# Two depooling stages written out in groups of four tiles

## The chip, the cores and the metric

The kernel runs on one core of one Trainium2 chip. The metric is the device time of one execution in microseconds. Engine names: PE (TensorE), DVE (VectorE), ACT (ScalarE), POOL (GpSimd), SP (SyncE, which issues the DMAs here).

## What is computed

The network has twelve blocks, in four layers of three, on an `x` of 128 sequences x 32 positions x 128 features; each block adds its result to `x`. Blocks `L0_xattn` (the first) and `L3_xattn` (the tenth) are the "depooling" blocks:

```python
def _hnet_depool(h, h_patch_full, patch_lens):
    ...
    _, s = jax.lax.associative_scan(comb, (a_b, u), axis=1)   # decaying sum over the patches
    depool = s.reshape(bsz, plen, D_MODEL)
    plug = jnp.clip(jnp.cumsum(boundary_mask, axis=1) - 1, 0, plen - 1)
    depool_out = depool[jnp.arange(bsz)[:, None], plug]       # one row per position
    return depool_out + h
h = rmsnorm(embeds, g_res)
h = jnp.einsum('bld,ed->ble', h, W_in) + b_in
h_patch = rmsnorm(patch_embeds, g_init)
return _hnet_depool(h, h_patch, patch_lens)
...
x = x + _L0_xattn_ref(_layernorm(x, axis=-1), ctx_2048, mask_BxS2_if0, L0_xattn_W_in, ...)
```

`embeds` is the layer-normalised `x`; `patch_embeds` comes from `ctx_2048` alone.

## The kernel before, in words

`x` stays in SBUF for the whole program as `core.x`, 32 tiles of 128 rows (4 sequences x 32 positions) by 128 features. A first piece of code, `start`, prepares what both depooling stages share: `core.ctx_n`, the normalised context rows, and `core.depool`, for each tile the 128x128 matrix that does scan and gather in one matmul. Then the twelve stages run one after another. Each has its own block of code per engine, and a barrier stands between two stages: no engine works ahead into the next one. Inside a stage the engines run their own queues in written order and meet only at semaphores. The profile cuts the leading `L0` or `L3` of a tile's name to `L`, so `L_xattn_patch` is that of either depooling stage, by its time.

A depooling stage, `depool_cross`, does for each tile: mean and variance (`dve_moments`, DVE lines L119 and L122); the inverse root, which is both normalisations in one, as four small operations on POOL (`pool_rstd`, L135, L138, L140, L142); `(x - mean) * rstd` on DVE (`dve_normalise`, L147), a 128x128 operation per tile; a transpose on PE (L153), copied by ACT out of PSUM four tiles at a time (L160); two matmuls per tile into the same PSUM region, `depool` matrix times `patch` (L417) and transposed tile times `w` (L418); and `x_b` plus that sum into `x` on DVE, four tiles at a time (L398). `patch` is `ctx_n * g_init`, on POOL (L365), and `x_b` is `x + b_in`, on POOL (L369); both treat four tiles (128x512) per instruction. ACT copies the matrices of four tiles into `mat` (L382) ahead of the matmuls.

The tiles go in four rounds of eight (`S = 8`), three in a hardware loop (`over_steps`) and the last written out. DVE and POOL wait at the start for all four loads (`w_in`, 64), and DVE first scales `w` by `g_res` (L388). Within a round POOL does `patch` twice, `x_b` twice and then the roots of the next round; DVE does the moments and the normalising of the next round and then this round's two additions.

A later stage, `lora_experts` (`L3_ffn`, called the expert stage below), is untouched by the change. It is written out in groups of four tiles and adds a bias in place on POOL (L2882).

Of the kernel before, what the change touches and what calls it, by code (L numbers as in the profile page):

```python
# [328 lines left out]
def depool_cross(core, name):  # L329

    nc, dram = core.nc, core.dram
    S, PACK = 8, 4
    with ExitStack() as st:
# [4 lines left out]
        x_b = sb("x_b", [P, S, D])  # L338
        g_init = sb("g_init", [P, D])
        mat = sb("mat", [P, S, P])  # L340
        patch = sb("patch", [P, S, D])
        front = Front(core, st, name, S, lambda s: core.psum[:, s // PACK, s % PACK * P:s % PACK * P + P], rms=True,
                      pack=PACK)
        out = lambda u: core.psum[:, 2 + u, :].rearrange("p (s d) -> p s d", d=D)
        w_in, w_done, copied, patch_done, x_b_done, out_done, added = (core.sem(f"{name}_{n}") for n in (
            "w_in", "w_done", "copied", "patch_done", "x_b_done", "out_done", "added"))
        block = st.enter_context(nc.Block())
        U = S // PACK

        @block.sync  # L350
        def _(sp):
            load(sp, [(w[:, :], dram[f"{name}_W_in_T"]), (g_res[:, :], dram[f"{name}_g_res"]),
                      (b_in[:, :], dram[f"{name}_b_in"].to_broadcast([P, D])),
                      (g_init[:, :], dram[f"{name}_g_init"][:, 0:D].to_broadcast([P, D]))], w_in)

        @block.gpsimd
        def _(pool):
            pool.wait_ge(w_in, 64)
            b4 = b_in[:, :].rearrange("p (s d) -> p s d", s=1).to_broadcast([P, PACK, D])
            g4 = g_init[:, :].rearrange("p (s d) -> p s d", s=1).to_broadcast([P, PACK, D])  # L360
            def step(it, more):
                for u in range(U):

                    pool.wait_ge(out_done, it * U + u + 1)
                    nc.gpsimd.tensor_tensor(patch[:, 4 * u:4 * u + 4, :], core.ctx_n[:, ds(it * S + 4 * u, PACK), :], g4,  # L365
                                            ALU.mult).then_inc(patch_done, 1)
                for u in range(U):
                    pool.wait_ge(added, it * U + u + 1)
                    nc.gpsimd.tensor_tensor(x_b[:, 4 * u:4 * u + 4, :], core.x[:, ds(it * S + 4 * u, PACK), :], b4,  # L369
                                            ALU.add).then_inc(x_b_done, 1)  # L370
                if more:
                    front.pool_rstd(pool, (it + 1) * S)
# [2761 lines left out]
```

## Time and profile before

| | us |
|---|---|
| median of 3 runs | 4280.81 (4277.31 to 4282.16) |
| the profiled execution | 4273.29 |
| its span, first to last instruction | 4271.1 |
| first depooling stage, first load to end of last addition | 63.15 to 116.20 |
| second depooling stage | 4044.84 to 4098.95 |

In the profile a time is counted from the span's start. Busy time of an engine leaves out waits; "idle before" an instruction, in brackets, names what ended the wait. The two depooling stages are 107 of 4271 us; PE is busy 81% of the whole span, DVE 63%, POOL 28%.

### The profile page before, as it was taken

Reading aid. Unit: us, or ns where it says so; the run is one execution under the profiler, and the core shown is the slowest. Engines: PE = TensorE matmul, PEld = TensorE weight load, DVE = VectorE, ACT = ScalarE, POOL = GpSimd, SP = SyncE. Lnnn points to the kernel's source line nnn. Section 1 sums busy time; section 2 is a strip of 40 time slices with the busy share of each in tenths; the row PEclk is TensorE's granted clock in tenths of the full one; section 3 lists DMA queues with packets and bytes.
Section 4 is the critical chain, followed back from the end, with each engine's and each line's share of the span. In section 5 each row is a group of like instructions: output and inputs, shape, how many; then the busy total and the mean of one; then the engine's idle time right before and its main releaser. Section 6 shows DMA issues by size and latency. Waiting matters only on the chain. (4 is left out here: it accounts for less than half of the span.)

```text
span 4271.1 us, 82785 instructions
## 1 busy us (share of the span) xinstructions
PE 3473.3 (81%) x26877; PEld 2960.9 (69%) x26885; DVE 2688.3 (63%) x7468; ACT 1765.1 (41%) x4503; POOL 1202.9 (28%) x1644
## 2 busy tenths in 40 slices
PE   3787788888868888777769999999999999872634
PEld 2676777777756666445559999999999999642334
DVE  6773888888857888564235545555555554477667
ACT  1230666666637777554113323333332332222542
POOL 2551766676623333202000000000000000153021
PEclk8995999999989999988669999999999999876666
DMA  3000000000012222100111111111111111162000
GB/s 84 4 0 32 1 0 0 0 0 0 0 32 71 77 75 75 41 5 0 31 39 46 51 40 50 46 45 45 45 51 40 50 46 46 32 108 47 2 0 22
DMA packets 262344, 147.46 MB, mean 35 GB/s; under 512 B 110327, under 2 KB 258763, under 8 KB 261614
## 3 DMA queue, kind: packets, MB, share of 16 engines
q1 hardware_dynamic: 257742, 140.55, 12.4%
q10 hardware_dynamic: 4512, 5.77, 0.6%
q8 instruction: 49, 0.80, 0.1%
q14 instruction: 41, 0.34, 0.0%
HBM read 131.82 MB, written 13.65 MB: 34 GB/s over the span
## 5 line engine op out<-in xcount | busy, mean ns | idle before, releaser
L901 PE MATMUL psum<-L_ffn_share,L_ffn_prob 128*128 128x128 f32 x4096 | 511.2, 284 | 141.5 <-DVE L_ffn_prob L830 141.5
L901 PEld LDWEIGHTS psum<-L_ffn_share,L_ffn_prob 128*128 128x128 f32 x4096 | 491.3, 198 | 173.5 <-DVE L_ffn_prob L830 141.9
L2074 ACT ACTIVATE L_xattn_prob<-psum,L_xattn_nmax 128x258 f32<-128x258 f32 x512 | 238.6, 471 | 677.3 <-DVE L_xattn_nmax L2109 677.3
L725 POOL TENSOR_TENSOR L_ffn_sums<-L_ffn_sims 128x1024 f32<-128x1024 f32 x256 | 485.5, 1911 | 107.6 <-DVE L_ffn_prob L830 107.3
L2186 PE MATMUL psum<-L_xattn_ctxT,L_xattn_q_ctx 128*128 128x257 f32 x2048 | 488.8, 381 | 0.0
L2224 PE MATMUL psum<-L_xattn_probT,L_xattn_ctx 128*128 128x256 f32 x2048 | 484.6, 380 | 1.7 <-DVE L_xattn_probT L2127 1.7
L830 DVE SCALAR_TENSOR_TENSOR L_ffn_prob<-L_ffn_sums,L_ffn_best,psum 128x512 f32<-128x512 f32 x512 | 358.2, 740 | 105.2 <-ACT psum L758 101.2
L2127 DVE COPY L_xattn_probT<-psum 128x512 f32<-128x512 f32 x256 | 176.9, 691 | 392.0 <-PE psum L2210 392.0
L2186 PEld LDWEIGHTS psum<-L_xattn_ctxT,L_xattn_q_ctx 128*128 128x128 f32 x2048 | 370.9, 191 | 48.2
L2049 POOL TENSOR_TENSOR L_xattn_z_var<-L_xattn_z_mv,L_xattn_z_eps 128x1 f32<-128x1 f32 x32 | 6.1, 190 | 1398.0 <-DVE L_xattn_z_mv L2141 1365.3
L2224 PEld LDWEIGHTS psum<-L_xattn_probT,L_xattn_ctx 128*128 128x128 f32 x2048 | 370.2, 191 | 42.0 <-ACT L_xattn_lastT L2085 2.2
L758 ACT ACTIVATE psum<-L_ffn_sums,L_ffn_bias 128x512 f32<-128x512 f32 x512 | 337.1, 683 | 136.2 <-DVE L_ffn_prob L830 136.1
L1189 ACT ACTIVATE L_xattn_prob<-psum,L_xattn_nmax 128x289 f32<-128x289 f32 x512 | 249.5, 500 | 125.5 <-DVE L_xattn_nmax L1216 125.5
L2090 ACT COPY L_xattn_mixed_ctx<-psum 128x512 f32<-128x512 f32 x256 | 149.7, 585 | 362.1 <-PE psum L2224 362.1
L2171 PEld LDWEIGHTS psum<-L_xattn_xnT,L_xattn_m_h 128*128 128x128 f32 x2048 | 273.3, 197 | 23.4 <-DVE L_xattn_q_ctx L2101 9.7
L2171 PE MATMUL psum<-L_xattn_xnT,L_xattn_m_h 128*128 (+1 forms) x2048 | 279.9, 281 | 8.6 <-DVE L_xattn_q_ctx L2101 7.0
L2195 PEld LDWEIGHTS psum<-L_xattn_u_h,L_xattn_mixed_ctx 128*128 128x128 f32 x2048 | 233.5, 192 | 2.9 <-ACT L_xattn_mixed_ctx L2090 1.1
L2195 PE MATMUL psum<-L_xattn_u_h,L_xattn_mixed_ctx 128*128 128x128 f32 x2048 | 233.9, 275 | 0.7 <-ACT L_xattn_mixed_ctx L2090 0.7
L1216 DVE TENSOR_REDUCE L_xattn_nmax<-psum 128x1 f32<-128x289 f32 x512 | 198.9, 450 | 45.9 <-PE psum L1256 45.8
L2101 DVE COPY L_xattn_q_ctx<-psum 128x512 f32<-128x512 f32 x256 | 174.7, 682 | 38.3 <-PE psum L2171 38.3
L2109 DVE TENSOR_REDUCE L_xattn_nmax<-psum 128x2 f32<-128x516 f32 x256 | 177.9, 695 | 20.5 <-issue 2.9
L2117 DVE TENSOR_SCALAR L_xattn_prob<-L_xattn_prob,L_xattn_total 128x256 f32<-128x256 f32 x512 | 158.5, 351 | 20.0
(426 smaller groups left out, 6629.0 us busy)
## 6 DMA issues: line engine op xcount, KB each, us to landing
L_xattn_ctxT<-ctx_T_dram SPq DMA_DIRECT2D x128, 257.0 KB, 2.8
L_xattn_ctx<-ctx_dram SPq DMA_DIRECT2D x128, 256.0 KB, 3.0
L_xattn_k_all<-ctx_T_dram SPq DMA_DIRECT2D x128, 128.5 KB, 2.1
L_xattn_v_all<-ctx_dram SPq DMA_DIRECT2D x128, 128.0 KB, 2.2
L_attn_qkv_scratch<-L_attn_qkv SPq DMA_DIRECT2D x24, 256.0 KB, 2.9
L_attn_rows<-L_attn_qkv_scratch SPq DMA_DIRECT2D x24, 256.0 KB, 5.3
start_raw<-ctx_dram ACTq DMA_DIRECT2D x16, 256.0 KB, 12.2
start_plug_all<-plug_scratch SPq DMA_DIRECT2D x1, 2048.0 KB, 6.7
```

What stands on the lines that cost most here:

```text
L725: nc.gpsimd.tensor_tensor(sums[:, h % RING, :, :], sx, sy, ALU.add).then_inc(summed, 1)
L758: nc.scalar.activation(raw_prob(k), half(sums[:, h % RING, :, :].rearrange("p i j -> p (i j)"), k), ACT.Exp, bias=bias[:, s, h:h + 1]).the ...
L830: nc.vector.scalar_tensor_tensor(half(prob[:, h % RING, :], k), half(sums[:, h % RING, :, :].rearrange("p i j -> p (i j)"), k), best[:, s, ...
L901: last = nc.tensor.matmul(pair(2 * s)[:, c * P:(c + 1) * P], prob[:, h % RING, c * P:(c + 1) * P], share[:, h % RING, :], start=(h == 0 an ...
L1189: ins = nc.scalar.activation(prob[:, b % 2, g, :], scores(g), ACT.Exp, bias=nmax[:, b % 2, g:g + 1], accum_out=total[:, b % 2, g:g + 1])
L1216: nc.vector.tensor_reduce(nmax[:, b % 2, g:g + 1], scores(g), X, ALU.max, negate=True).then_inc(maxed, 1)
L2074: ins = nc.scalar.activation(prob[:, s, g, :], scores(s)[:, g, :], ACT.Exp, bias=nmax[:, s, g:g + 1], accum_out=total[:, s, g:g + 1])
L2109: nc.vector.tensor_reduce(nmax[:, u % 2, :], scores(u % 2), X, ALU.max, negate=True).then_inc(maxed, 1)
L2171: last = nc.tensor.matmul(Q[:, i * P:(i + 1) * P], m_h[:, 4 * j + i, c * P:(c + 1) * P], tokens(t), start=True, stop=True)
L2186: last = nc.tensor.matmul(scores(s)[:, g, 0:CTX], q_ctx[:, p, c, b, h:h + 4, :].rearrange("p h n -> p (h n)"), ctxT[:, b, c, :], start=(c ...
L2195: nc.tensor.matmul(OUT, mixed_ctx[:, c, h, :], u_h[:, c, h, :], start=(c + h == 0), stop=False)
L2224: last = nc.tensor.matmul(dst, ctx[:, b, k, c * P:(c + 1) * P], probT[:, s, k, :], start=(k == 0), stop=(k == 1))
```

## The change

Only `depool_cross` is edited; both depooling stages use it. Eight groups of four tiles are written out without a loop. `front` has slots for all 32 tiles, so no buffer of the normalised tiles is used twice. The loads come in another order on two semaphores: `g_init` and `b_in` (`rows_in`, for POOL), then `w` and `g_res` (`w_in`, for DVE). DVE takes moments at once and scales `w` behind the normalising of group 0. POOL takes the roots of groups 0 and 1 by themselves and later ones over pairs of groups; it adds the bias to `x` in place once the group is normalised, and `x_b` is gone. PE reads `core.depool` in place, so `mat` and ACT's copies are gone. PE transposes group g+1 ahead of the product of group g, and group g's addition stands on DVE behind the normalising of group g+2.

```diff
-    S, PACK = 8, 4
+    S = 4
+    GROUPS = TILES // S
...
+        patch = sb("patch", [P, TILES, D])
+        xnT = sb("xnT", [D, 3, S, P])
+        front = Front(core, st, name, TILES, None, transposed=False, rms=True)
+        turn_bank = lambda g: core.psum[:, g % 2, :].rearrange("p (s w) -> p s w", s=S)
+        out_bank = lambda g: core.psum[:, 2 + g % 2, :].rearrange("p (s d) -> p s d", d=D)
...
+            load(sp, [(g_init[:, :], dram[f"{name}_g_init"][:, 0:D].to_broadcast([P, D])),
+                      (b_in[:, :], dram[f"{name}_b_in"].to_broadcast([P, D]))], rows_in)
+            load(sp, [(w[:, :], dram[f"{name}_W_in_T"]), (g_res[:, :], dram[f"{name}_g_res"])], w_in)
...
+            def patches(g):
+                nc.gpsimd.tensor_tensor(patch[:, g * S:(g + 1) * S, :], core.ctx_n[:, g * S:(g + 1) * S, :], over(g_init),
+                                        ALU.mult).then_inc(patch_done, 1)
+
+            def add_bias(g):
+                pool.wait_ge(front.normed, (g + 1) * S)
+                nc.gpsimd.tensor_tensor(x_of(g), x_of(g), over(b_in), ALU.add).then_inc(biased, 1)
+
+            front.pool_rstd(pool, 0, only=tiles(0))
+            front.pool_rstd(pool, 0, only=tiles(1))
+            pool.wait_ge(rows_in, 32)
+            patches(0)
+            patches(1)
+            for g in range(2, GROUPS, 2):
+                front.pool_rstd(pool, 0, only=pair(g))
+                add_bias(g - 2)
+                patches(g)
+                add_bias(g - 1)
+                patches(g + 1)
+            add_bias(GROUPS - 2)
+            add_bias(GROUPS - 1)
...
+            for g in range(GROUPS):
+                act.wait_ge(front.turned, (g + 1) * S)
+                if g >= 3:
+                    act.wait_ge(out_done, g - 2)
+                nc.scalar.copy(xnT[:, g % 3, :, :], turn_bank(g)).then_inc(xnT_done, 1)
...
-            dve.wait_ge(w_in, 64)
...
+            def add(g):
+                dve.wait_ge(out_done, g + 1)
+                dve.wait_ge(biased, g + 1)
+                nc.vector.tensor_tensor(x_of(g), x_of(g), out_bank(g), ALU.add).then_inc(added, 1)
+
+            front.dve_moments(dve, 0, only=tiles(0))
+            front.dve_moments(dve, 0, only=tiles(1))
+            front.dve_normalise(dve, 0, only=tiles(0))
+            dve.wait_ge(w_in, 32)
             nc.vector.tensor_scalar(w[:, :], w[:, :], g_res[:, :], None, ALU.mult).then_inc(w_done, 1)
...
+            for g in range(1, GROUPS + 2):
+                if g % 2 and g + 2 < GROUPS:
+                    front.dve_moments(dve, 0, only=pair(g + 1))
+                if g < GROUPS:
+                    front.dve_normalise(dve, 0, only=tiles(g))
+                if g >= 2:
+                    add(g - 2)
...
+            def turn(g):
+                if g >= 2:
+                    pe.wait_ge(xnT_done, g - 1)
+                for s in range(S):
+                    pe.wait_ge(front.normed, g * S + s + 1)
+                    nc.tensor.transpose(turn_bank(g)[:, s, :], front.xn[:, g * S + s, :],
+                                        core.c("ident")).then_inc(front.turned, 1)
+
+            def out(g):
+                pe.wait_ge(patch_done, g + 1)
+                if g >= 2:
+                    pe.wait_ge(added, g - 1)
+                pe.wait_ge(xnT_done, g + 1)
+                for s in range(S):
+                    nc.tensor.matmul(out_bank(g)[:, s, :], core.depool[:, g * S + s, :], patch[:, g * S + s, :], start=True,
+                                     stop=False)
+                    last = nc.tensor.matmul(out_bank(g)[:, s, :], xnT[:, g % 3, s, :], w[:, :], start=False, stop=True)
+                last.then_inc(out_done, 1)
+
+            turn(0)
             pe.wait_ge(w_done, 1)
+            for g in range(GROUPS):
+                if g + 1 < GROUPS:
+                    turn(g + 1)
+                out(g)
```

How the rows move. On DVE at the head of the stage, before: scaling of `w` (L388), moments and normalising of eight tiles, then the loop.

```order
L388 TENSOR_SCALAR L_xattn_w<-L_xattn_w,L_xattn_g_res 128x128
L119 BN_STATS L_xattn_front_stats_sb<-x_sb 128x6 x8
L122 BN_AGGR L_xattn_front_mv_sb<-L_xattn_front_stats_sb 128x2 x8
L147 TENSOR_SCALAR L_xattn_front_xn_sb<-x_sb,L_xattn_front_mv_sb,L_xattn_front_rstd_sb 128x128 x8
L179 UNCONDITIONAL_BRANCH
```

The same place in the changed kernel (L403 scales `w`, L397 is the addition into `x`):

```order
L119 BN_STATS L_xattn_front_stats_sb<-x_sb 128x6 x4
L122 BN_AGGR L_xattn_front_mv_sb<-L_xattn_front_stats_sb 128x2 x4
L119 BN_STATS L_xattn_front_stats_sb<-x_sb 128x6 x4
L122 BN_AGGR L_xattn_front_mv_sb<-L_xattn_front_stats_sb 128x2 x4
L147 TENSOR_SCALAR L_xattn_front_xn_sb<-x_sb,L_xattn_front_mv_sb,L_xattn_front_rstd_sb 128x128 x4
L403 TENSOR_SCALAR L_xattn_w<-L_xattn_w,L_xattn_g_res 128x128
L119 BN_STATS L_xattn_front_stats_sb<-x_sb 128x6 x8
L122 BN_AGGR L_xattn_front_mv_sb<-L_xattn_front_stats_sb 128x2 x8
L147 TENSOR_SCALAR L_xattn_front_xn_sb<-x_sb,L_xattn_front_mv_sb,L_xattn_front_rstd_sb 128x128 x8
L397 TENSOR_TENSOR x_sb<-x_sb,psum 128x512
```

Moments of two groups now stand ahead of everything, and `w` behind group 0; the eight L147 in a row are groups 1 and 2, with no addition between them.

On POOL, one pass of the loop before: `patch` (L365) and `x_b` (L369) of a round, then the roots of the next.

```order
L365 TENSOR_TENSOR L_xattn_patch<-ctx_n,L_xattn_g_init 128x512
L364 REGISTER_ALU
L365 ISA
L365 TENSOR_TENSOR L_xattn_patch<-ctx_n,L_xattn_g_init 128x512
L369 REGISTER_ALU
L369 TENSOR_TENSOR L_xattn_x_b<-x_sb,L_xattn_b_in 128x512
L369 REGISTER_ALU
L369 TENSOR_TENSOR L_xattn_x_b<-x_sb,L_xattn_b_in 128x512
L134 ISA
L135 TENSOR_TENSOR L_xattn_front_var_sb<-L_xattn_front_mv_sb,eps 128x8
```

In the changed kernel, from the root over groups 2 and 3 to the next root (L363 is `patches`, L368 `add_bias`):

```order
L142 TENSOR_TENSOR L_xattn_front_rstd_sb<-L_xattn_front_var_sb,minus_half 128x8
L368 TENSOR_TENSOR x_sb<-x_sb,L_xattn_b_in 128x512
L363 TENSOR_TENSOR L_xattn_patch<-ctx_n,L_xattn_g_init 128x512
L368 TENSOR_TENSOR x_sb<-x_sb,L_xattn_b_in 128x512
L363 TENSOR_TENSOR L_xattn_patch<-ctx_n,L_xattn_g_init 128x512
L135 TENSOR_TENSOR L_xattn_front_var_sb<-L_xattn_front_mv_sb,eps 128x8
```

The four operations of 128x512 are still between two roots, but the two on `x` now concern the groups before this pair, in place.

## Rows read from the trace of the kernel before

**Rows 1.** Windows by round, first stage: us, busy us of each engine (instructions), TensorE clock.
```profile
63.15:73.00 9.85, 0.00 (x0) 0.00 (x0) 2.57 (x17) 1.14 (x2) 2.21 (x4) 0.50 0.08 20
73.00:84.35 11.35, 7.71 (x39) 6.42 (x40) 8.26 (x24) 1.79 (x3) 7.15 (x9) 0.59 0.00 0
...
105.57:116.20 10.63, 7.49 (x40) 6.11 (x40) 6.53 (x12) 1.39 (x3) 4.97 (x5) 0.84 0.00 0
```

**Rows 2.** Timeline of DVE and POOL, first stage: start us, us, engine, line, operation.
```profile
67.46 0.29 DVE L388 TENSOR_SCALAR L_xattn_w<-L_xattn_w,L_xattn_g_res 128x128 f32<-128x128 f32 x1 [4.57 <-DMA L_xattn_g_init<-L_xattn_g_init_dram]
...
70.36 0.20 POOL L135 TENSOR_TENSOR L_xattn_front_var_sb<-L_xattn_front_mv_sb,eps 128x8 f32<-128x8 f32 x1 [11.92 <-DVE L_xattn_front_mv_sb L122]
...
73.00 2.48 POOL L365 TENSOR_TENSOR L_xattn_patch<-ctx_n,L_xattn_g_init 128x512 f32<-128x512 f32 x2
73.07 5.97 DVE L147 TENSOR_SCALAR L_xattn_front_xn_sb<-x_sb,L_xattn_front_mv_sb,L_xattn_front_rstd_sb 128x128 f32<-128x128 f32 x8 [2.87 <-POOL L_xattn_front_rstd_sb L142]
...
75.44 2.49 POOL L369 TENSOR_TENSOR L_xattn_x_b<-x_sb,L_xattn_b_in 128x512 f32<-128x512 f32 x2
...
84.50 3.96 DVE L147 TENSOR_SCALAR L_xattn_front_xn_sb<-x_sb,L_xattn_front_mv_sb,L_xattn_front_rstd_sb 128x128 f32 x8 [2.88 <-POOL L_xattn_front_rstd_sb L142]
```

**Rows 3.** Normalising instructions (L147), first stage: duration ns min/median/max, first and last start.
```profile
L147 DVE TENSOR_SCALAR L_xattn_front_xn_sb<-x_sb,L_xattn_front_mv_sb,L_xattn_front_rstd_sb x32: 332/335/1303, 73.1 to 109.3; 128x128 f32 x24, 128x128 f32<-128x128 f32 x8
```

**Rows 4.** Timeline, later rounds of the first stage, and the start of the next stage.
```profile
89.22 2.49 POOL L369 TENSOR_TENSOR L_xattn_x_b<-x_sb,L_xattn_b_in 128x512 f32<-128x512 f32 x2 [2.38 <-DVE x_sb L398]
...
89.87 1.64 DVE L119 BATCH_NORM_STATS2 L_xattn_front_stats_sb<-x_sb 128x6 f32 x8 [0.21 <-issue]
...
110.33 0.80 PE L417 MATMUL psum<-L_xattn_patch,L_xattn_mat 128*128 128x128 f32 x2
...
113.72 0.69 DVE L398 TENSOR_TENSOR x_sb<-L_xattn_x_b,psum 128x512 f32<-128x512 f32 x1 [2.85 <-PE psum L418]
...
115.51 0.69 DVE L398 TENSOR_TENSOR x_sb<-L_xattn_x_b,psum 128x512 f32<-128x512 f32 x1 [1.10 <-PE psum L418]
116.47 0.33 SPq L167 DMA_DIRECT2D L_attn_w_qk<-L_attn_Wqk_dram  x1
...
116.57 0.29 DVE L119 BATCH_NORM_STATS2 L_attn_front_stats_sb<-x_sb 128x6 f32<-128x128 f32 x1 [0.38 <-PEq L333]
```

**Rows 5.** Timeline of the expert stage (L3_ffn, last of the program), DVE and POOL.
```profile
4201.42 1.08 DVE L119 BATCH_NORM_STATS2 L_ffn_front_stats_sb<-x_sb 128x6 f32<-128x128 f32 x4 [0.37 <-PEq L2718]
...
4204.43 1.11 DVE L147 TENSOR_SCALAR L_ffn_front_xn_sb<-x_sb,L_ffn_front_mv_sb,L_ffn_front_rstd_sb 128x128 f32<-128x128 f32 x4
...
4215.15 1.46 DVE L147 TENSOR_SCALAR L_ffn_front_xn_sb<-x_sb,L_ffn_front_mv_sb,L_ffn_front_rstd_sb 128x128 f32<-128x128 f32 x2 [0.34 <-POOL L_ffn_front_rstd_sb L142]
...
4203.38 1.01 POOL L142 TENSOR_TENSOR L_ffn_front_rstd_sb<-L_ffn_front_var_sb,minus_half 128x4 f32<-128x4 f32 x1
...
4204.80 1.10 POOL L142 TENSOR_TENSOR L_ffn_front_rstd_sb<-L_ffn_front_var_sb,minus_half 128x4 f32<-128x4 f32 x1
...
4215.01 1.26 POOL L2882 TENSOR_TENSOR x_sb<-x_sb,L_ffn_b_lin 128x512 f32<-128x512 f32 x1
```

**Rows 6.** DMA issues in the first stage's head: line, size, us from issue to landing.
```profile
L_xattn_g_res<-L_xattn_g_res_dram SPq DMA_DIRECT2D x1, 0.5 KB, 2.0
```

**Rows 7.** Windows of PE: us, busy us (instructions), granted clock, DMA share, GB/s.
```profile
99.72:102.60 2.88, 2.88 (x13) 0.50 0.00 0
...
113.10:115.50 2.40, 2.37 (x21) 1.00 0.00 0
```

**Rows 8.** Timeline of the head of the second depooling stage.
```profile
4049.28 0.29 DVE L388 TENSOR_SCALAR L_xattn_w<-L_xattn_w,L_xattn_g_res 128x128 f32<-128x128 f32 x1 [5.71 <-DMA L_xattn_g_init<-L_xattn_g_init_dram]
...
4052.71 0.19 POOL L135 TENSOR_TENSOR L_xattn_front_var_sb<-L_xattn_front_mv_sb,eps 128x8 f32<-128x8 f32 x1 [49.42 <-DVE L_xattn_front_mv_sb L122]
```

**Rows 9.** Windows by round, second stage (columns as in the first group).
```profile
4044.84:4055.41 10.57, 0.00 (x0) 0.00 (x0) 2.57 (x17) 1.14 (x2) 2.27 (x4) 0.52 0.08 19
...
4088.00:4098.95 10.95, 7.67 (x40) 6.38 (x40) 6.54 (x12) 1.79 (x3) 4.98 (x5) 0.84 0.00 1
```

More of the change, by code:

```diff
@@ L347, in depool_cross @@
         block = st.enter_context(nc.Block())
-        U = S // PACK
+        tiles = lambda g: range(g * S, (g + 1) * S)
+        pair = lambda g: range(g * S, (g + 2) * S)
+        x_of = lambda g: core.x[:, g * S:(g + 1) * S, :]
         @block.sync
         def _(sp):
-            load(sp, [(w[:, :], dram[f"{name}_W_in_T"]), (g_res[:, :], dram[f"{name}_g_res"]),
-                      (b_in[:, :], dram[f"{name}_b_in"].to_broadcast([P, D])),
-                      (g_init[:, :], dram[f"{name}_g_init"][:, 0:D].to_broadcast([P, D]))], w_in)
+            load(sp, [(g_init[:, :], dram[f"{name}_g_init"][:, 0:D].to_broadcast([P, D])),
+                      (b_in[:, :], dram[f"{name}_b_in"].to_broadcast([P, D]))], rows_in)
+            load(sp, [(w[:, :], dram[f"{name}_W_in_T"]), (g_res[:, :], dram[f"{name}_g_res"])], w_in)
@@ L356, in _ @@
         @block.gpsimd
         def _(pool):
[L358 to L372, printed above, removed]
@@ L374, in _ @@
-            front.pool_rstd(pool, 0)
-            over_steps(pool, TILES // S, step)
+            over = lambda t: t[:, :].rearrange("p (s d) -> p s d", s=1).to_broadcast([P, S, D])
+            def patches(g):
[4 more added lines that the diff above has]
+                nc.gpsimd.tensor_tensor(x_of(g), x_of(g), over(b_in), ALU.add).then_inc(biased, 1)
@@ L385, in _ @@
         @block.vector
         def _(dve):
-            dve.wait_ge(w_in, 64)
-            nc.vector.tensor_scalar(w[:, :], w[:, :], g_res[:, :], None, ALU.mult).then_inc(w_done, 1)
-            def step(it, more):
-                if more:
-                    front.dve_moments(dve, (it + 1) * S)
-                    dve.wait_ge(front.turned, (it + 1) * S)
-                    front.dve_normalise(dve, (it + 1) * S)
-                for u in range(U):
-                    dve.wait_ge(out_done, (it + 1) * U + u + 1)
-                    x = core.x[:, ds(it * S + 4 * u, PACK), :]
-                    dve.wait_ge(x_b_done, it * U + u + 1)
-                    nc.vector.tensor_tensor(x, x_b[:, 4 * u:4 * u + 4, :], out(u), ALU.add).then_inc(added, 1)
@@ L407, in _ @@
-            pe.sem_inc(added, U)
-            pe.wait_ge(w_done, 1)
-            with pe.Fori(0, TILES // S) as it:
-                front.pe_transpose(pe, it * S)
-                for u in range(U):
-                    pe.wait_ge(added, it * U + u + 1)
-                    pe.wait_ge(copied, it * U + u + 1)
-                    pe.wait_ge(patch_done, it * U + u + 1)
-                    pe.wait_ge(front.xnT_done, it * S + 4 * u + 4)
-                    for s in range(4 * u, 4 * u + 4):
-                        nc.tensor.matmul(out(u)[:, s % 4, :], mat[:, s, :], patch[:, s, :], start=True, stop=False)
-                        last = nc.tensor.matmul(out(u)[:, s % 4, :], front.xnT[:, s, :], w[:, :], start=False, stop=True)
-                    last.then_inc(out_done, 1)
+            def turn(g):
[5 more added lines that the diff above has]
+                                        core.c("ident")).then_inc(front.turned, 1)
```

19 lines of the change are left out of this document (2 added, 17 removed).

## The prediction

> **What bounds the kernel now.** Every stage starts behind a barrier, so only time inside the two depooling stages can move. I read the windows by round first [rows 1]. The first stage lasts from 63.15 to 116.20: 53.05 us, of which 9.85 are a head, 11.35 the first round (from one start of `patch` on POOL to the next), 10.63 the last, which leaves 10.61 for each of the two between. In no round is an engine near full (DVE 8.26 of 11.35), so this is a chain of waits. The head [rows 2] shows DVE doing nothing until 67.46, when the last of four loads has landed; then come moments, the four steps of the inverse root on POOL (from 70.36), and at 73.00 `patch`.
>
> The round is a loop of two engines: the root waits for the moments, the normalising (DVE L147) waits for the root, and the next moments stand behind it on DVE. See L147 in the first round: eight tiles take 5.97 us, beside four POOL operations of 128x512 that run without a gap from 73.00 to 77.93. In the second round, beside two such operations, they take 3.96. The shortest is 0.332 us, the longest 1.303, a POOL operation's length [rows 3], and four tiles beside small POOL operations take 1.11 (4204.43), which is 0.27 from start to start. So while POOL works through 128x512 operands one tile gets through per operation, and the rest follow at 0.27. The count fits twice: 4 x 1.24 + 4 x 0.27 = 6.0, and 2 x 1.24 + 6 x 0.27 = 4.1. Moments are not held: beside the two `x_b` operations of 89.22, eight tiles take 1.64 us in all [rows 4], little more than one of them.
>
> **The change, from POOL's queue.** I write t for the first moment at which DVE can work in a stage, 0.10 us behind the first load, as in the stage that follows (116.57 against 116.47 [rows 4]): 63.25 and 4044.94. P is the start of the 128x512 operations on POOL behind a root over a pair of groups.
>
> *Head.* In the expert stage the first moments of four start at 4201.42 and the root's last step at 4203.38, 0.35 behind its first [rows 5]. So the first root starts at t+1.6; it costs 3 x 0.35 + 1.01 = 2.06, the second as much: they end at t+3.7 and t+5.75. `patches` 0 and 1 add 2.48: t+8.2. Their rows are issued 0.9 us earlier or more than the load that had landed by 67.46, so they are there by t+4. DVE normalises group 0 until t+4.85 and then wants `w` and `g_res`; the latter, issued at about t+1.2, needs 2.0 us [rows 6] and is covered by 1.6. Scaling and the moments of groups 2 and 3 end at t+7.5, under `patches`. The root over this pair takes 2.64 (70.36 to 73.00): P2 = t+10.8, that is 74.05, against 73.00 for the first P of before.
>
> *Rounds.* Behind each pair's root POOL has bias, patch, bias, patch, with nothing to wait for: the biases need tiles normalised a round earlier. That is 4.97 us without a gap, and in it DVE wants the four tiles of the even group. Before, round one alone met four operations, later ones two. By the count above all four tiles are held, to P+5.03. In the expert stage this very operation, `x` plus bias in place behind the same wait, starts at 4215.01, ahead of L147 at 4215.15, whose first two tiles take 1.46 us [rows 5]. So POOL gets in first. Then come the addition (0.67), the moments of the next pair (0.08 + 1.64 + 0.08 + 0.64), 0.09 to POOL and 2.64 for its root: 5.03 + 0.67 + 2.44 + 0.09 + 2.64 = 10.87, and 10.84 since an operation starts 0.03 before its predecessor's recorded end. Before: 10.61. Both handle eight tiles, so writing the pipeline out gains nothing in a round. The odd group's tiles (1.11) and its addition run beside the next root.
>
> *Tail.* From P6: tiles of group 6 done at 5.03; their transposes 0.35; PE has held back group 5's product behind them: 3.35 us at granted clock 0.50, that is 1.2 GHz, as from 110.33 to the addition at 113.72 [rows 4, 7]; transposes of group 7, 0.9; products of 6 and 7 at 1.79 each at clock 1.00, 2.4 GHz, as between the additions of 113.72 and 115.51; last addition 0.73: 13.96 us. Before it was 10.63 from the last P, with eight tiles to normalise but two groups, not three, left for PE.
>
> *Off the path.* ACT's copies of the matrices go; ACT is busy 1.79 of 11.35 us [rows 1], so this is 0, and would stay 0 unless PE had its tiles first. PE gets one new order: group g's product stands behind the transposes of g+1. Group 1's, at the slow clock, ends at P+8.7 and its addition is wanted at P+9.2; were this cover of 0.5 us gone, group 4's tiles still have 1.0 us until the next P. Bias in place costs what `x_b` did (1.26 against 2.49 for two).
>
> *Sum.* First stage: head +1.05, one round less -11.35 (three roots over pairs where there were four), two rounds +0.46, tail +3.33: -6.5 us. Second stage: from `w` at 4049.28 to POOL's first operation at 4052.71 it took 3.43 us [rows 8], against 2.90 in the first; I keep those 0.5. Head (10.57 before [rows 9]) +0.83, round -11.35, rounds +0.46, tail 13.96 against 10.95, +3.01: -7.1. Together -13.6. The profiled execution took 4273.29 us, of which 2.2 lie outside its span of 4271.1; it would become 4259.7. The median stood 7.5 above it, so I forecast 4280.8 - 13.6 = 4267.2 us, -0.32%.
>
> **Bounds of what before does not show.** PE's clock when group 5's product starts: before, a round's first product ran at 0.50 although transposes had just gone ahead [rows 7], and I take the same. High here, the tail is 1.6 us shorter per stage: 4264. Low for group 6 too: 4270. The head may lose 1 us per stage to a late `g_res`, or gain 0.5 once if POOL is on time. The runs of before spread over 4.8 us.
>
> **Rivals.**
> *DVE slips ahead of POOL (9%).* If the tiles were not held, a round would be POOL's 2.64 + 4.97 = 7.6, so -6.5 in two rounds, and the tail 3.8 shorter: another -10.3 per stage, 4247. For it: the order of two ready engines is a matter of 0.1 us. Against it: in both places where both stand ready, 73.00 and 4215.01, POOL has won.
>
> *The root holds the tiles too (9%).* I let tiles run freely beside the root; the four of 4204.43 do, while the root's last step beside them took 1.10 instead of 1.01 [rows 5]. If instead each of POOL's four steps let one tile through and was held by one, the root would cost 1.1 us more in the head and in two rounds, and group 0 would delay the moments by some tenths: 3.5 us a stage, 4274, within 0.2%. The Trainium skill, SBUF — State Buffer, section "Who interferes with whom", has this rule: whoever issues first, GpSimd or a VectorE instruction in a 2-port mode, keeps the shared pair "for the whole instruction". By that rule the 3.5 us would come; the trace agrees with it for 128x512 operations (1.303 us) and not for a root over four columns (1.11 for four tiles).
>
> *Straight code must be fetched (4%), the slower side.* Loops repeat their code; now every group's code is new on DVE, POOL and PE. POOL's 0.5 us at 4052.71, with no releaser but moments long done, may be such a fetch. Were it 0.52 us for each of three engines and 16 groups, 48 stalls on the path would cost 25 us: 4292. From 27 stalls the gain is gone, from 43 the kernel is slower by 0.2%. Against it: the expert stage is written out too, and the chain of its rows from 4201.42 to 4204.80 has no such hole. The Trainium skill, Runtime: NRT & Kernel Launch, section "Instruction fetch mechanics", calls the cost of crossing into the next block of straight code mostly hidden; no run here shows that cost.
>
> *The change doesn't do what it says (4%).* DVE's early start is worth nothing if the head stays bound elsewhere, and the tail could grow by another slow product with its transposes: 4 us per stage given back, 4275, no measurable change.
>
> **How the numbers follow.** The forecast case has 74%. What a measurement of this kernel can tell from no change is about 0.2%, 8.6 us. Range 4256 to 4276: below it lies the first rival, above it the fetch stalls and a little of the last; the middle holds PE's clock, `g_res` and the spread of medians. Faster: most of the 74, the 9 of the first rival: 0.81. Same: 0.15. Slower: 0.04.
>
> **What would show it.** DVE's first moments within 0.2 us of the first load, and `w` scaled without a wait. Four POOL operations without a gap behind each pair's root, beside them L147 at about 4.9 us for four tiles, and 1.1 for odd groups. P to P 10.8 us. Behind the last P three groups' products on PE, the first at clock 0.50. Stage lengths 46.5 and 47. The forecast is wrong if P to P is near 7.6, if odd groups' tiles are long, or if idle time with no releaser appears on DVE, POOL or PE.

## The result, and the profile after

The changed kernel took 4270.03 us (median of 16 runs, 4265.83 to 4276.65), the kernel before 4278.46 us in as many runs beside it (4271.87 to 4282.16). The ratio is 0.9983, with a 95% interval of 0.9975 to 0.999: faster by 0.17%, just short of the 0.2% that I had taken for the least that can be told from no change, and inside the predicted range. The gain is 8.4 us where 13.6 were forecast. The two stages show where it fell short. Windows by round of the first depooling stage of the changed kernel, with columns as in [rows 1], cut at the starts of the 128x512 operations behind each pair's root:

```profile
62.56:73.45 10.89, 3.68 (x15) 3.03 (x16) 7.82 (x41) 1.17 (x2) 8.11 (x14) 0.50 0.07 18
73.45:84.44 10.99, 9.20 (x45) 8.22 (x44) 9.46 (x26) 1.17 (x2) 7.36 (x9) 0.53 0.00 0
84.44:95.43 10.99, 7.37 (x47) 6.21 (x46) 9.44 (x26) 1.17 (x2) 7.36 (x10) 0.84 0.00 1
95.43:108.99 13.56, 9.18 (x61) 8.26 (x59) 9.20 (x12) 1.17 (x2) 7.46 (x7) 0.87 0.01 2
```

The same windows of the second stage, which answer to [rows 9]:

```profile
4047.38:4064.98 17.60, 3.67 (x15) 3.03 (x16) 7.83 (x41) 1.17 (x2) 8.15 (x14) 0.58 0.05 12
4064.98:4075.96 10.98, 8.88 (x51) 7.83 (x49) 9.42 (x26) 1.17 (x2) 7.35 (x9) 0.75 0.01 1
4075.96:4086.94 10.98, 7.13 (x43) 6.11 (x41) 9.43 (x26) 1.17 (x2) 7.34 (x9) 0.84 0.00 1
4086.94:4101.64 14.70, 10.13 (x59) 9.21 (x57) 9.21 (x12) 1.17 (x2) 7.47 (x7) 0.77 0.00 1
```

The first stage went from 53.05 to 46.43 us, as forecast (46.5). The second took 54.26 us, where it had taken 54.11: no gain. Its rounds are those of the first stage, its tail is 1.1 us longer, and its head is 17.60 us long instead of 10.89. The timeline of that head, beside [rows 8] (start us, us, engine, line, operation, and in brackets the idle time ahead and what ended it):

```profile
4047.38 0.35 SPq L167 DMA_DIRECT2D L_xattn_g_init<-L_xattn_g_init_dram  x1
...
4048.43 0.38 DVE L122 BATCH_NORM_AGGREGATE L_xattn_front_mv_sb<-L_xattn_front_stats_sb 128x2 f32<-128x6 f32 x4
...
4049.85 0.38 DVE L122 BATCH_NORM_AGGREGATE L_xattn_front_mv_sb<-L_xattn_front_stats_sb 128x2 f32<-128x6 f32 x4
...
4055.56 0.20 POOL L135 TENSOR_TENSOR L_xattn_front_var_sb<-L_xattn_front_mv_sb,eps 128x4 f32<-128x4 f32 x1 [49.74 <-issue]
...
4057.68 1.12 DVE L147 TENSOR_SCALAR L_xattn_front_xn_sb<-x_sb,L_xattn_front_mv_sb,L_xattn_front_rstd_sb 128x128 f32<-128x128 f32 x4 [7.46 <-POOL L_xattn_front_rstd_sb L142]
```

The moments of both first groups are done at 4050.23, the first group's at 4048.81. Yet POOL starts its root at 4055.56, 8.18 us behind the stage's first load, and the profile names nothing that it waited for ("issue"). In the first stage the same instruction follows its moments at once, 1.51 us behind the first load:

```profile
62.67 0.87 DVE L119 BATCH_NORM_STATS2 L_xattn_front_stats_sb<-x_sb 128x6 f32<-128x128 f32 x4 [0.36 <-PEq L202]
...
64.07 0.20 POOL L135 TENSOR_TENSOR L_xattn_front_var_sb<-L_xattn_front_mv_sb,eps 128x4 f32<-128x4 f32 x1 [6.23 <-DVE L_xattn_front_mv_sb L122]
...
67.19 0.28 DVE L403 TENSOR_SCALAR L_xattn_w<-L_xattn_w,L_xattn_g_res 128x128 f32<-128x128 f32 x1
...
70.75 0.20 POOL L135 TENSOR_TENSOR L_xattn_front_var_sb<-L_xattn_front_mv_sb,eps 128x8 f32<-128x8 f32 x1
```

So 6.67 us of the second stage are a late POOL. Before, the same operation stood 7.87 us behind the first load (4052.71 against 4044.84), but there the moments ended only at 4052.03. In the first stage before, POOL started 0.15 us behind the end of the moments (70.36 against 70.21); here it started 0.68 us behind it. So about 0.5 us of POOL's delay was visible, and the rest lay hidden.

### The profile page after: what moved, and what is told of

The parts are those of the page before. It is cut to its first block and busy times, and to the rows that moved or that the text cites. A ratio compares the mean times of both kernels' runs of the same rounds, so it can differ in the third digit from the quotient of the medians.

```text
span 4274.9 us, 82465 instructions
## 1 busy us (share of the span) xinstructions
PE 3485.5 (82%) x26885; PEld 2971.9 (70%) x26885; DVE 2697.9 (63%) x7468; ACT 1757.4 (41%) x4487; POOL 1209.6 (28%) x1652
```

## The experiments

**Theory S**: behind the quantised stage, whose last POOL work is two all-reduces over the partitions, POOL needs some 7 to 8 us to get ready for ordinary tensor operations. It starts on this when the next such instruction comes up in its queue, behind the barrier. In the list of POOL's instructions two entries `ISA` without operands stand between the two kinds. The one of L91 clears semaphores between stages; the one of L135 stands directly ahead of the root, and the trace has a row for it (below, under "What the delay is"). From the changed kernel (before, the same entries stand at the same places):

```
L2578 ISA L_ffn_most<-L_ffn_peaks 128x1
L2532 UNCONDITIONAL_BRANCH
L91 ISA
L358 UNCONDITIONAL_BRANCH
L135 ISA
L135 TENSOR_TENSOR L_xattn_front_var_sb<-L_xattn_front_mv_sb,eps 128x4
```

The rivals: it is a matter of the moments' timing (theory M), or chance, or POOL must only be woken, or the new code brings it, or something behind the barrier does, such as the clearing of semaphores or a fetch of new code (theory F).

"Stage" below is the time from its first load to the next stage's first load, in the profiled execution; POOL is its first tensor operation behind the second stage's first load. Each group of ratios was measured beside the kernel before, on one chip.

| kernel | first stage | second | POOL | ratio (95%) |
|---|---|---|---|---|
| before | 53.32 | 54.38 | 7.87 | |
| changed | 46.69 | 54.53 | 8.18 | 0.9983 (0.9975 to 0.999) |
| e0, changed again | 46.64 | 54.30 | 8.19 | 0.9989 (0.998 to 0.9998) |
| e1, small op early | 47.69 | 46.41 | 1.52 | 0.9977 (0.9967 to 0.9988) |
| e2, before + small op | 54.36 | 53.34 | 7.17 | 1.0003 (0.9994 to 1.0013) |
| e3, weights first | 50.35 | 54.58 | 8.23 | 0.9993 (0.9984 to 1.0003) |
| e4, tiles ahead of biases | 43.80 | 47.22 | 7.56 | 0.9968 (0.9957 to 0.9979) |
| e5, e1 and e4 | 44.13 | 42.69 | 1.51 | 0.9945 (0.9931 to 0.9959) |
| e6, first stage only | 46.56 | 54.08 | 8.08 | 0.9987 (0.9978 to 0.9996) |
| e7, second stage only | 53.66 | 53.24 | 8.26 | 1.0002 (0.9993 to 1.0011) |
| e8, e5 and the tail's tiles | 39.48 | 39.41 | 1.51 | 0.9936 (0.9923 to 0.995) |
| e9, odd product first | 44.96 | 53.37 | 8.16 | 0.9981 (0.9971 to 0.999) |
| e10, e8 and e9 | 39.45 | 39.36 | 1.51 | 0.9944 (0.9931 to 0.9958) |
| e11, small op late | 46.41 | 53.07 | 7.93 | 0.9983 (0.9973 to 0.9993) |

**e0: the changed kernel once more.**

> The changed kernel once more, to see what repeats. In its first profile the first depooling stage took 46.4 us (53.05 before), the second 54.3 (54.1 before), since POOL's first operation there came 6.7 us behind the moments; the rotary stage between them took 232.0 us against 222.7, with the granted clock of PE lower in several windows. If POOL's lateness is built into the program it repeats within 0.2 us; if it was chance it goes. The rotary stage's 9 us I take for chance: it should come out elsewhere between 222 and 233. The ratio to before should lie near 0.998.

POOL is late by the same amount (8.19), so it is not chance. In e4, whose stage has the same head, it starts after 7.56 us, so the delay is not the same to the tenth in every run.

**e1: a small POOL operation directly behind the all-reduces.**

```diff
+        scrap = sb("scrap", [P, 1])
...
             nc.gpsimd.partition_all_reduce(most[:, 3:4], peaks[:, 3:4], P,
                                            bass.bass_isa.ReduceOp.max).then_inc(most_h, 1)
+            nc.gpsimd.tensor_tensor(scrap[:, :], core.eps[:, :], core.half[:, :], ALU.mult)
```

> A one-column POOL operation is added behind the last all-reduce of the stage ahead of the second depooling stage, where POOL is idle for 40 us. Theory S (switch): an instruction that makes POOL ready for ordinary operations again after an all-reduce stands just ahead of its next ordinary operation, costs 7 to 8 us, and is now on the path; the added operation draws it forward. Then POOL's first root starts within 0.2 us of the moments, the second stage takes 46.5 to 47.2 us, and the kernel is 6.5 to 7.5 us faster than the changed one. Theory F (fetch of new code, or the clearing of semaphores, behind the barrier): nothing moves, second stage 54.3 us.

POOL's timeline, from the last all-reduce into the second depooling stage:

```profile
4002.72 0.37 POOL L2579 PARTITION_ALL_REDUCE L_ffn_most<-L_ffn_peaks  x1 [69.17 <-DVE L_ffn_peaks L2672]
4009.89 0.18 POOL L2581 TENSOR_TENSOR L_ffn_scrap<-eps,minus_half 128x1 f32<-128x1 f32 x1 [6.80 <-issue]
4047.82 0.20 POOL L135 TENSOR_TENSOR L_xattn_front_var_sb<-L_xattn_front_mv_sb,eps 128x4 f32<-128x4 f32 x1 [37.75 <-DVE L_xattn_front_mv_sb L122]
```

The idle time without a releaser has moved to the small operation (6.80 us), where POOL has nothing else to do for 38 us. The root now names its real releaser, the moments, and comes 1.52 us behind the first load. The second stage takes 46.41 us, 8.1 less than in the changed kernel; 6.7 of it are POOL, the rest is the tail (13.55 against 14.97 to the next stage's first load). Since the delay now passes ahead of the barrier and the root behind it is on time, nothing behind the barrier causes it, and theory F falls.

In device time the gain was smaller than the expected 6.5 to 7.5 us: the median is 4264.72 us, against 4267.59 for the changed kernel measured beside it (e0), 2.9 us less, and the intervals of the two ratios overlap. In the profiled execution the first stage's tail was 1.1 us longer than in the changed kernel, at PE's low clock, but the tail of one execution doesn't explain a median of nine. That the 6.7 us are gone is shown by the second stage's own length; that they reach the kernel's time in full is not shown by this run alone.

**e11: the same operation, but behind the barrier.**

```diff
+        scrap = sb("scrap", [P, 1])
...
         def _(pool):
...
+            nc.gpsimd.tensor_tensor(scrap[:, :], core.eps[:, :], core.half[:, :], ALU.mult)
```

> The changed kernel with the same small POOL operation as in e1_small_op_early, but as POOL's first instruction inside each depooling stage, behind the barrier and ahead of the first root, with nothing to wait for. Theory S (POOL starts to get ready for tensor operations when its first instruction of the stage comes up, behind the barrier, and needs until about 8 us behind the stage's first load): the small operation itself ends only 7.6 to 8.3 us behind the first load, the root stands behind it, the second stage stays at 54 to 55 us and the ratio at 0.9985. Rival (POOL must only be woken by any operation that doesn't wait for DVE): the small operation runs within 1 us of the first load, the root at 1.5 us, the second stage is 46.5 us and the ratio 0.9975.

```profile
4043.18 0.35 SPq L167 DMA_DIRECT2D L_xattn_g_init<-L_xattn_g_init_dram  x1
...
4051.11 0.18 POOL L371 TENSOR_TENSOR L_xattn_scrap<-eps,minus_half 128x1 f32<-128x1 f32 x1 [51.09 <-issue]
4051.26 0.19 POOL L135 TENSOR_TENSOR L_xattn_front_var_sb<-L_xattn_front_mv_sb,eps 128x4 f32<-128x4 f32 x1
```

An operation that waits for nothing starts 7.93 us behind the first load. So the delay falls on the first tensor operation behind the all-reduces, also on one that waits for nothing; where it stands decides whether it costs anything. The second stage, 53.07 us, is 0.9 below the 54 to 55 that I expected; its tail was 13.61 us against the changed kernel's 14.97.

**e2: the small operation in the kernel before.** Same edit as e1.

> The kernel before, with the same small POOL operation behind the second all-reduce of the quantised stage as in the run e1_small_op_early. Theory S (POOL needs about 8 us from the barrier until its first tensor operation, and before this lay behind the late load of w and the moments but for half a microsecond): the second stage goes from 54.4 to about 53.9 us, as the first (53.3) has it, and the kernel's time does not change (ratio within 0.9985 to 1.0005). Rival (the small operation saves its 8 us in any kernel, for instance by making the barrier come earlier): the second stage about 46.5 us and the kernel at 0.998.

The second stage is 1.04 us shorter, 0.70 of it in POOL's start, and the kernel's time did not change. (The first stage, which the edit doesn't touch, came out 1.04 us longer, so a difference of this size in one profile means little.) POOL still starts 7.17 us behind the first load, but now it is the moments that it waits for: the cover itself is this long.

**e3: loads first, as before.** DVE waits for `w` and `g_res` ahead of the first moments.

```diff
+            dve.wait_ge(w_in, 32)
             front.dve_moments(dve, 0, only=tiles(0))
             front.dve_moments(dve, 0, only=tiles(1))
             front.dve_normalise(dve, 0, only=tiles(0))
-            dve.wait_ge(w_in, 32)
```

> One part of the change undone: DVE waits for the weights ahead of the first moments, as before. First stage: the fourth load lands 3.5 to 4.0 us behind the start, so the head and the stage grow by about that: 50.0 to 50.6 us. Second stage under theory S: POOL is not ready until 8.2 us behind the stage's first load, and the moments of group 0 end at 5.5, still earlier; no change, 54.3 us. If instead POOL's lateness runs from the moment the moments are done (theory M), the second stage also grows by 4, to 58.

```profile
4048.60 0.35 SPq L167 DMA_DIRECT2D L_xattn_g_init<-L_xattn_g_init_dram  x1
...
4052.56 0.87 DVE L119 BATCH_NORM_STATS2 L_xattn_front_stats_sb<-x_sb 128x6 f32<-128x128 f32 x4 [5.24 <-DMA L_xattn_g_res<-L_xattn_g_res_dram]
...
4056.83 0.19 POOL L135 TENSOR_TENSOR L_xattn_front_var_sb<-L_xattn_front_mv_sb,eps 128x4 f32<-128x4 f32 x1 [49.80 <-issue]
```

In the first stage the early moments are worth 3.7 us (50.35 against 46.69). In the second they are worth nothing: moments 3.9 us later, POOL at 8.23 as ever. Theory M expected 58 us there; it took 54.58.

**e6 and e7: the new code in one stage, the loop in the other.**

> The new code in the first depooling stage, the old loop in the second. Theory S: the whole gain of the change sits in the first stage: 46.6 us there and 54.4 in the second, the kernel as fast as with both changed (ratio to the kernel before 0.9985, -6.7 us). Rival (the second stage's new code does gain, and something else of the program pays it back): about half of the changed kernel's gain, ratio 0.999 to 1.0.

> The old loop in the first depooling stage, the new code in the second. Theory S: first stage 53.3 us, second 54.4 (POOL's first tensor operation 8.2 us behind the stage's first load), ratio to the kernel before 1.000 within 0.0007. Rival (the late POOL of the changed kernel comes from the new code in the first stage, which leaves other things loaded): POOL on time, second stage about 47 us, ratio 0.9985.

The whole gain sits in the first stage (0.9987), and the second alone gives none that can be told (1.0002, 0.9993 to 1.0011). In e6 the root of the second stage, at 8.08, waited for the moments, as in the kernel before. With the old loop in the first stage POOL is just as late in the second (8.26), so the new code in the first stage doesn't cause it. e7's second stage of 53.24 us is 1.1 below my expectation, from a shorter tail.

**e4: POOL lets the tiles go first.** Behind each pair's root POOL waits for the even group's tiles before it starts its four operations.

```diff
                 front.pool_rstd(pool, 0, only=pair(g))
+                pool.wait_ge(front.normed, (g + 1) * S)
                 add_bias(g - 2)
```

> POOL waits for the tiles of the even group before its four 128x512 operations. Theory L (a tile waits out each POOL operation, and this sets the round): the four tiles take 1.1 us instead of 4.95, the next moments are ready at P+4.3, POOL's four operations run from P+1.2 to P+6.2 and its root follows: a round of 8.9 us instead of 10.98, the tail 11.4 instead of 13.6, each stage 6.2 to 6.6 us shorter, the kernel 12 to 13 us faster than the changed one. Odd tiles now meet POOL and take 3 to 5 us. Rival: the round is set by the number of steps in the chain and not by who goes first; then POOL's four operations, now behind the tiles, lengthen it to 11 or more.

DVE and POOL in the first round, and DVE in the tail:

```profile
73.67 1.12 DVE L147 TENSOR_SCALAR L_xattn_front_xn_sb<-x_sb,L_xattn_front_mv_sb,L_xattn_front_rstd_sb 128x128 f32<-128x128 f32 x4 [1.88 <-POOL L_xattn_front_rstd_sb L142]
74.86 1.27 POOL L368 TENSOR_TENSOR x_sb<-x_sb,L_xattn_b_in 128x512 f32<-128x512 f32 x1 [1.23 <-DVE L_xattn_front_xn_sb L147]
...
94.96 3.99 DVE L147 TENSOR_SCALAR L_xattn_front_xn_sb<-x_sb,L_xattn_front_mv_sb,L_xattn_front_rstd_sb 128x128 f32<-128x128 f32 x4
```

Four tiles take 1.12 us instead of 4.96, POOL waits 1.23 for them, and a round falls from 10.99 to 8.89 (74.86 to 83.75). In the tail the last group's four tiles are now held instead (3.99), and PE's product behind them ran at the low clock: from the last P to the next stage's first load it took 13.9 us in the first stage, where I had expected some 11.4, and 11.2 in the second, at the high clock. The waits in between cost as well: POOL's wait ahead of the first pair moved P2 back by 1.25 us (12.14 behind the first load instead of 10.89). So the stages gained 2.9 and 7.3 us where I had expected 6.2 to 6.6 each, and the kernel's median was 5.8 us below e0's (4261.76 against 4267.59) where I had expected 12 to 13. The four tiles and the round did what theory L says; the kernel's gain did not come out. Apart from the last group, odd tiles took 1.36 us and not the 3 to 5 expected.

**e5: e1 and e4 together.**

> The changed kernel with the small POOL operation early and with each bias addition on POOL waiting for its group's normalised tiles. If the two are independent, as theory S and the hold of the tiles by 128x512 operations have it: first stage 43.8 us, second 39.5 to 41 (54.4 less 7.9 less 6.2 to 7.1), against the kernel before 53.3 and 54.4: 23 us in all, ratio about 0.9945. Rival (both pull at the same wait, so that only the larger counts in the second stage): second stage about 46.5 us, ratio about 0.996.

Both count: ratio 0.9945, as expected. The second stage (42.69) missed its expectation by 1.7 us or more. I had taken it from e4's second stage, whose last 6 us ran at the high clock, and here a product ran at the low one. The last windows of e4's second stage (columns as above):

```profile
4085.39:4088.39 3.00, 2.10 (x18) 1.92 (x19) 1.63 (x2) 0.59 (x1) 2.22 (x2) 1.00 0.02 5
4088.39:4091.39 3.00, 2.00 (x18) 1.81 (x17) 1.37 (x2) 0.00 (x0) 0.00 (x0) 1.00 0.00 0
```

and of e5's:

```profile
4078.49:4081.49 3.00, 3.00 (x17) 3.00 (x16) 0.19 (x2) 0.43 (x1) 0.77 (x1) 0.53 0.00 0
4081.49:4084.49 3.00, 2.02 (x16) 1.82 (x14) 1.20 (x2) 0.00 (x0) 0.00 (x0) 0.90 0.00 0
```

**e8: the last group's tiles go first too.**

```diff
                 patches(g)
+                if g == GROUPS - 2:
+                    pool.wait_ge(front.normed, (g + 2) * S)
                 add_bias(g - 1)
```

> The kernel of e5_both, in which POOL also waits for the tiles of the last group before the bias addition of group 5. In e5_both these four tiles took 4.16 us (first stage, 95.55 to 99.71) beside 128x512 operations. Theory H (one tile per such operation, free otherwise): 1.1 to 1.4 us, PE's transposes and its last two products start 2.9 us sooner, and a stage gets shorter by 3 to 4.4 us: 40 to 41 us and 39 to 40 us, ratio to the kernel before about 0.993. Rival (the clock of PE decides the tail, and a product that starts sooner runs slower): the tiles are short but a stage gains under 1 us, ratio 0.9945 as for e5_both.

```profile
96.33 1.11 DVE L147 TENSOR_SCALAR L_xattn_front_xn_sb<-x_sb,L_xattn_front_mv_sb,L_xattn_front_rstd_sb 128x128 f32<-128x128 f32 x4
...
99.98 2.50 POOL L368 TENSOR_TENSOR x_sb<-x_sb,L_xattn_b_in 128x512 f32<-128x512 f32 x2
...
102.58 0.69 DVE L400 TENSOR_TENSOR x_sb<-x_sb,psum 128x512 f32<-128x512 f32 x1 [0.54 <-POOL x_sb L368]
```

```profile
93.98:103.54 9.56, 6.96 (x54) 6.12 (x53) 3.78 (x8) 1.17 (x2) 7.46 (x6) 1.00 0.00 1
```

The first stage's tail is 9.56 us long, with PE at clock 1.00 throughout, and now POOL's last bias sets its end. The stages are 4.7 and 3.3 us shorter than in e5, where I had expected 3 to 4.4. Not all of it is the tiles: in the first stage's tail PE was busy 9.63 us in e5, at a mean clock of 0.76, and 6.96 us here, for the same 54 recorded matmuls. No run separates the two. This is the fastest kernel of the study: 4245.5 us against 4273.75, 28 us where the change as made gave 8.

**e9: PE's order for odd groups swapped.**

```diff
             for g in range(GROUPS):
+                if g % 2:
+                    out(g)
                 if g + 1 < GROUPS:
                     turn(g + 1)
-                out(g)
+                if g % 2 == 0:
+                    out(g)
```

> The changed kernel with PE's order swapped for odd groups: the product of group 5 stands ahead of the transposes of group 6 (the same for 1 and 3). It has its data 7 us sooner. Order theory (as my prediction priced the tail: group 5's product is held back by its place and costs 3.35 us there): from the last P to the stage's end 10.2 us in place of 13.6, -6.8 us in the kernel, ratio to the kernel before about 0.9967. Clock theory (the first product behind a pause of PE runs at the low clock, whichever group's it is): group 6's product takes the 3.3 us instead and the tail shrinks by 0 to 1 us per stage; ratio 0.998, as the changed kernel. The second stage's late POOL stays in both.

PE's windows in the first stage, the products of groups 4 and 5, then of 6 and 7 (us, PE busy, clock):

```profile
94.12:100.14 6.02, 6.02 (x33) 0.57 0.01 3
103.16:106.90 3.74, 3.74 (x33) 1.00 0.00 0
```

Neither theory was right alone. The slow products now lie mostly under the held tiles of group 6, and group 6's own ran at 1.00, which the clock theory denied. But the tail shrank by 1.6 us here (13.82 to 12.19) and by 1.2 in the second stage, where a product ran slow again, not by 3.4. My 10.2 had left out the tiles and transposes of group 7, which stand behind those of group 6. The ratio, 0.9981, can't be told from that of the changed kernel.

**e10: e8 with the order of e9.**

> e8_tail_tiles_first with the order of PE of e9_odd_product_first. In e8 the product of group 6 waits for the tiles of the last group, not for PE, so PE's order is worth 0 to 1 us per stage: ratio within 0.0005 of that of e8. Rival (PE's queue sets the tail once the tiles are early): 2 to 3 us per stage more, ratio about 0.992.

The stages are those of e8 to within 0.05 us. The ratios of 0.9944 and 0.9936 differ by more than I gave them, but their intervals overlap and the stages don't differ: PE's order is worth nothing that these profiles show once the tiles are early.

## Why the prediction was right and where it was wrong

**Head of the first stage: right.** POOL's first root came 1.4 us behind DVE's first moment, forecast 1.6; `w` was scaled at 67.19 with no wait; P2 was at t+10.78 (73.45), forecast 10.8.

**Rounds: right in mechanism, 0.15 us short.** The even group's tiles took 4.96 us beside the four operations, forecast 5.0; the odd group's 1.09:

```profile
73.52 4.96 DVE L147 TENSOR_SCALAR L_xattn_front_xn_sb<-x_sb,L_xattn_front_mv_sb,L_xattn_front_rstd_sb 128x128 f32<-128x128 f32 x4 [1.88 <-POOL L_xattn_front_rstd_sb L142]
```

In e4 the same tiles took 1.12 as soon as POOL stood still, so the hold is shown, not only counted. The round was 10.99 instead of 10.84. The 0.15 is the root: its second step, beside the odd group's tiles, took 0.37 us instead of 0.20. From POOL's timeline in the changed kernel:

```profile
81.96 0.37 POOL L138 TENSOR_TENSOR L_xattn_front_var_sb<-L_xattn_front_var_sb,eps 128x8 f32<-128x8 f32 x1
```

This is what there is of the rival "the root holds the tiles too": some tenths a round, not 1.1 us. The rule that it named (the Trainium skill, SBUF — State Buffer, "Who interferes with whom") fits the 128x512 operations (one tile in each, 1.24 us apart), and fits the small operations hardly at all.

**Tail of the first stage: right, the forecast 0.4 us too long** (13.96 against 13.56; the terms add up to 13.94, and from 110.33 to 113.72 it is 3.39 us, not 3.35: slips of hundredths). Three products behind the last P, the first at the low clock. PE's windows, group 5's product and what follows (us, busy, clock):

```profile
100.66:103.90 3.24, 3.24 (x17) 0.53 0.00 0
103.90:108.20 4.30, 4.30 (x37) 0.96 0.00 0
```

The forecast put the first product's 3.35 us down to PE's order. e9, with the order swapped, got back 1.6 and 1.2 us and not all of it; e8, with early tiles, has a tail 4.3 us shorter, 1.2 of it paid back as POOL's wait ahead of the last P.

**Second stage: wrong.** The step that failed is "Second stage: from `w` at 4049.28 to POOL's first operation at 4052.71 it took 3.43 us, against 2.90 in the first; I keep those 0.5". I read the 0.5 us as the size of a delay. They were the end of one that lasted until 7.87 us behind the first load, which loads and moments had covered, and the change took away the cover. In my own terms, I costed the early moments at a gain and did not ask what else they had been hiding. The price of 6.67 us is the difference of POOL's starts, 8.18 and 1.51. e1 gets it back, e11 and e3 show that it depends neither on the moments nor on the work asked for, and e2 that it was hidden before. Put in place of the 0.5 that the forecast of 47 contained, it makes 53.2. The rest of the 54.26 is the tail (14.70 against 13.96), where more of PE's work ran at the low clock than I had counted, and 0.14 in each of the two rounds.

Two rivals touch on it. "The change doesn't do what it says" (4%) names this outcome, that the early start is worth nothing if the head stays bound elsewhere; in the second stage it did. And I had named the sign of it, in the rival on fetched code ("POOL's 0.5 us at 4052.71, with no releaser but moments long done, may be such a fetch"), but priced it as many stalls in straight code. The first stage, straight code as well, has none. It is one stall, at one place; e7 shows it with the loop in the first stage, and the kernel before, with the loop in both, had it as well.

**What the delay is** the trace says in part. POOL's instruction queue has rows in it. For the changed kernel, the lines of the root (L135) and of the drain directly behind it (L137, the program's order to wait for the root's end):

```profile
L135 POOLq MODIFY_POOL_CONFIG  x2: 11/11/11, 4047.5 to 4047.5; - x2
L135 POOL TENSOR_TENSOR L_xattn_front_var_sb<-L_xattn_front_mv_sb,eps x1: 195/195/195, 4055.6 to 4055.6; 128x4 f32<-128x4 f32 x1
...
L137 POOLq DRAIN  x1: 6946/6946/6946, 4048.9 to 4048.9; - x1
```

Two rows `MODIFY_POOL_CONFIG` of 11 ns stand 0.1 us behind the stage's first load; this is the `ISA` entry of L135. The queue reached the drain at 4048.9, when group 0's moments were done, so it had let the root through by then; yet the root ran 6.7 us later. In e1 the same two rows stand directly behind the last all-reduce, and the small operation follows 6.8 us later:

```profile
L2581 POOLq MODIFY_POOL_CONFIG  x2: 85/85/85, 4003.0 to 4003.1; - x2
L2581 POOL TENSOR_TENSOR L_ffn_scrap<-eps,minus_half x1: 180/180/180, 4009.9 to 4009.9; 128x1 f32<-128x1 f32 x1
```

In all runs the delay runs from these rows: 6.8 to 7.1 us where they stand ahead of the barrier (e1, e2, e5, e8, e10), 7.4 to 8.1 where they stand behind it and the operation doesn't wait for moments (changed, e0, e3, e4, e7, e9, e11). Why it is longer there is open. The rows alone cost nothing: such a pair stands at two other places of the changed kernel, and the operation follows within 0.2 us, for instance

```profile
L1467 POOLq MODIFY_POOL_CONFIG  x2: 13/13/13, 1776.2 to 1776.2; - x2
L1467 POOL TENSOR_SCALAR L_attn_below<-L_attn_b_dt x1: 194/194/194, 1776.3 to 1776.3; 128x2 f32<-128x2 f32 x1
```

A fourth pair stands ahead of the first all-reduce, 7.07 us before it in every run; but there POOL waits for DVE's peaks, which end 0.1 us before it starts, so whether the way to the all-reduces costs the same can't be told.

What is done in the delay has no row. Over the nine microseconds from 4047 to 4056 the DMA engines move the stage's loads and then nothing, before POOL starts (busy tenths in 40 slices), and in e1, from 4002 to 4011, they move nothing at all:

```profile
DMA  0000001123356335100000000000000000000000
```

The Trainium skill, GPSIMD Engine Reference, section "2.1 Instruction dispatch", says that the first call to a freshly loaded kernel costs approximately 6 us "with no visible profile instruction". The 6.8 us of e1 agree with it in kind and are 0.8 us more; behind the barrier it is up to 2 us more, and here the measured time is the one to count with. That a switch back from the all-reduces to plain tensor operations counts as such a load, and that POOL's code is what is loaded, is an inference from the rows and their place; no run shows it.

**The sum.** Stages in the profiled executions: -6.6 and +0.15, against -6.5 and -7.1. The medians differ by 8.4 us; the 1.9 over the stages' 6.5 lie within the interval (0.0008 of 4278 is 3.4 us).

The time of 4270.03 us lies nearer to the forecast 4267.2 than the gain does to its own, and that is luck: the forecast started from a median of three runs, 4280.8 us, and sixteen runs gave 4278.46. From these it would have been 4264.9, 5.2 us too low, and in the profiled stages the gain was half of the forecast one (6.5 of 13.6). By the prediction's own measure of 0.2% the outcome is "same", to which it gave 0.15, though the interval lies wholly below 1.

## What to carry to other kernels

An idle time that ends a little behind its named releaser is the visible end of something that may be much longer: measure the engine's first operation from the barrier, not from its releaser, before making the releaser earlier. When POOL's tensor operations follow a stage with all-reduces over partitions, try a scrap tensor operation right behind the last of them, where POOL is idle: here it took 6.7 us out of a stage, and nothing where the delay was covered (e2). And let a short dependent burst on DVE go ahead of POOL's wide operations, by a wait on POOL: here this cost 1.2 us of POOL per pair and gave 3.8 us to DVE, 2.1 us per round, but little in the tail until the last group's tiles went first too.

## What the runs showed of the hardware

The clock granted to PE is the largest unsteadiness that I found in this kernel. The stage behind the first depooling stage is the same in all kernels; its windows, before and changed (us, PE busy, clock):

```profile
116.47:339.14 222.67, 180.84 (x2208) 0.92 0.01 2
```

```profile
109.25:341.22 231.97, 190.11 (x2208) 0.87 0.01 2
```

The same 2208 matmuls take 9.3 us more at a mean clock of 0.87. It isn't the change: in e0, the changed kernel again, the stage took 222.55 us at 0.92, in e8 222.89 and in e1 229.48. That the profiled execution of the changed kernel was the slowest of its 16 (4276.65) has this for its main part, as far as one profile can say. Within a depooling stage, too, the tail of one and the same kernel (changed kernel and e1, from the last P to the next stage's first load) came out between 13.6 and 15.0 us, by how many products fell into the low clock. So a stage's time in a single profile carries about 1 us of this, and smaller differences in the table mean nothing by themselves.
